# Second block: ones, low parts, sums and statistics placed anew; last routing: scaling on ScalarE

## The reference

```
x = x + _L0_xattn_ref(_layernorm(x), ctx, ctx, mask, Wq, Wk, Wv, Wo)      # 16 heads
x = x + _L0_ffn_ref(_layernorm(x), gate_w, fc_w, proj_w)                  # best 2 of 8 experts, gelu
x = x + _L1_xattn_ref(_layernorm(x), ctx, ctx, Wq, bq, Wk, bk, Wv, bv)    # one head
x = x + _L1_ffn_ref(_layernorm(x), Wr, br, W1, b1, W2, b2)                # 8 experts, dense, gated by the best 2
x = x + _L2_xattn_ref(_layernorm(x), ctx, Wq, Wkv, Wout, bout)
x = x + _L2_ffn_ref(_layernorm(x), w1, conv_w, conv_b, w2)                # ternary weights, convolution
x = x + _L3_xattn_ref(_layernorm(x), ctx, ctx, mask, Wq, bq, ..., Wo, bo)
x = x + _L3_ffn_ref(_layernorm(x), w_gate, w_gate_up, w_down)             # best 2 of 8 experts, silu(g) * u
```

## Time and profile before

| | us |
|---|---|
| runs | 600.94, 597.98, 601.21 |
| median | 600.94 |
| the profiled execution | 604.28 |
| its span, first to last instruction | 602.5 |

### The profile page before, as it was taken

How to read it: one execution, slowest core, us unless ns; L and a number is a source line. 1 busy time by engine, 2 the same in 40 slices (tenths; PEclk the granted TensorE clock), 3 DMA queues, 4 the chain that set the end, 5 groups by cost and what they waited for, 6 DMA issues and landing times.

```text
span 602.5 us, 12300 instructions
## 1 busy us (share of the span) xinstructions
PE 543.9 (90%) x3794; PEld 458.7 (76%) x3809; DVE 401.4 (67%) x1443; ACT 239.3 (40%) x551; POOL 280.1 (46%) x521
## 2 busy tenths in 40 slices
PE   5999984769999799999999999999996897999992
PEld 3678744669997498889987877767773697899992
DVE  8978853333356795465789899988887654555573
ACT  3555503345553543434444334365521222343330
POOL 4474378867657106910000050664526688644332
PEclk9999865999998999989999999999998798999997
DMA  9999012222253100000000450004001222111233
GB/s 302 377 328 274 13 53 67 68 62 75 71 167 104 64 1 1 2 0 1 1 2 0 141 140 2 1 1 141 1 1 45 67 70 58 54 46 52 79 110 122
DMA packets 48153, 47.65 MB, mean 79 GB/s; under 512 B 6471, under 2 KB 37604, under 8 KB 47943
## 3 DMA queue, kind: packets, MB, share of 16 engines
q1 hardware_dynamic: 43558, 37.68, 21.3%
q0 software_dynamic: 4544, 9.38, 4.7%
HBM read 27.53 MB, written 19.51 MB: 78 GB/s over the span
## 4 chain that ended last, share of the span: by engine, by line
PE 58%; DVE 18%; issue 11%; SPq 8%; ACT 2%; another core or an unknown queue 1%; DMA 1%; DVEq 0%; POOL 0%; POOLq 0%; ACTq 0%
PE bank L2453 18%; PE bank L2466 10%; PE bank L2027 7%; SPq L474 4%; SPq L468 2%; PE bank L2016 2%; PE bank L2017 2%; PE bank L2018 2%; PE bank L2441 2%; PE bank L2310 2%; PE bank L2223 2%; SPq L463 1%; PE bank L2268 1%; DVE X L1602 1%
## 5 line engine op out<-in xcount | busy, mean ns | idle before, releaser
L2453 PE MATMUL bank<-xT,wcur 128*128 128x128 f32 x936 | 122.7, 282 | 14.1 <-ACT xT L903 10.5
L2453 PEld LDWEIGHTS bank<-xT,wcur 128*128 128x128 f32 x936 | 114.6, 197 | 17.3 <-issue 9.4
L706 POOL DMA_INDIRECT yt<-Y,dest_i x62 | 60.3, 973 | 59.6 <-ACT Y L919 39.3
L645 POOL TENSOR_SCALAR var_eps<-mv 128x4 f32<-128x4 f32 (+2 forms) x12 | 2.9, 238 | 165.4 <-DVEq L1846 93.5
L690 POOL DMA_INDIRECT xw<-XW,slot_i x64 | 63.1, 986 | 24.6 <-issue 13.0
L1458 DVE COPY wcur<-WA 128x512 f32 x78 | 35.2, 452 | 51.1 <-PE bank L2453 37.3
L987 ACT ACTIVATE hT<-bank,b_cols 128x512 f32<-128x512 f32 x64 | 44.0, 688 | 61.4 <-PE bank L2018 60.8
L2027 PE MATMUL bank<-WC,hT 128*128 128x128 f32 x512 | 64.4, 281 | 0.0
L2027 PEld LDWEIGHTS bank<-WC,hT 128*128 128x128 f32 x512 | 62.0, 196 | 1.6 <-issue 0.2
L1473 DVE TENSOR_TENSOR hT<-gb,bank 128x512 f32<-128x512 f32 x39 | 26.8, 688 | 50.5 <-ACT gb L908 44.2
L1602 DVE SCALAR_TENSOR_TENSOR X<-bank,G,X 128x128 f32<-128x128 f32 x128 | 35.9, 345 | 29.9 <-PE bank L2027 23.5
(11 more groups left out here) (407 smaller groups left out, 1185.6 us busy)
## 6 DMA issues: line engine op xcount, KB each, us to landing
xw<-pad_rows SPq DMA_DIRECT2D x34, 260.0 KB, 4.2
xrow<-xw SPq DMA_DIRECT2D x78, 65.0 KB
WA<-in_fc_dram SPq DMA_DIRECT2D x16, 256.0 KB, 4.3
YT<-yt SPq DMA_DIRECT2D x16, 256.0 KB, 3.2
WA<-in_pj_dram SPq DMA_DIRECT2D x8, 256.0 KB, 5.9
WB<-in_fc_dram SPq DMA_DIRECT2D x8, 256.0 KB, 5.3
WB<-in_pj_dram SPq DMA_DIRECT2D x8, 256.0 KB, 6.5
X<-in_x_dram SPq DMA_DIRECT2D x2, 512.0 KB, 4.2
```

What stands on the lines that cost most here:

```text
L706: pool.indirect_dma_start(out=yt_dram, out_offset=bass.IndirectOffsetOnAxis(ap=dest_i[:, t:t + 1], axis=0), in_=y_slot(layer, t), in_offse ...
L2453: ins = pe.matmul(dst, wcur[:, s4, at:at + P], xT[s4 % 2][:, :], start=True, stop=True)
```

## The change

- TensorE issues `warm(4, 3)` at the start of `second_block`.
- `low(i)` reads PSUM and the high part, and waits for `high(i)` alone; both high copies come first, and `whole(i)` waits for `low(i)`.
- In `second_block` VectorE takes the four statistics of a batch right after adding its values.
- `weight_sums` goes from ahead of the first gates to unit 3 on VectorE, and from unit 3 to unit 6 on TensorE; `weight_scales` goes from unit 3 to unit 6, and TensorE's wait for it from unit 5 to unit 9.
- In the last routing ScalarE makes half 1's scaled tiles: `from_mean` (mean minus token) before the first exponentials, `times_root` (times the root, which GpSimd now makes with a negative sign) after them and before the two copies out of PSUM. VectorE's `ln_scaled(half(1))` stays in layer 0 alone.
- The first `warm(9, 4)` of that router becomes `warm(3, 4)`.
- Two semaphores for the masks' loads become one, `in_masks` (left out of the diff below).

```diff
@@ -640,15 +640,16 @@
-            def root(columns):
+            def root(columns, sign=1.0):
                 v, a, b = var_eps[:, columns], y_squared[:, columns], minus_half_vyy[:, columns]
...
                 for k in range(3):
+                    to = sign if k == 2 else 1.0
                     link(pool.tensor_tensor(a, y, y, ALU.mult))
                     link(pool.tensor_tensor(b, v, a, ALU.mult))
-                    link(pool.tensor_scalar(b, b, -0.5, 1.5, ALU.mult, ALU.add))
+                    link(pool.tensor_scalar(b, b, -0.5 * to, 1.5 * to, ALU.mult, ALU.add))
                     link(pool.tensor_tensor(rstd[:, columns], b, y, ALU.mult))
@@ -665,7 +666,7 @@
                 pool.wait_ge(mv_ready, 4 + 8 * a)
-                root(slice(GT, TILES))
+                root(slice(GT, TILES), (1.0, -1.0)[a])
                 pool.sem_inc(rstd_ready, 1)
@@ -857,6 +858,18 @@
+            def from_mean():
+                act.wait_ge(mv_ready, 12)
+                act.wait_ge(xn_ready, 3 * TILES + GT)
+                for t in range(GT, TILES):
+                    act.activation(XNR[:, t, :], X[:, t, :], ACT.Identity, bias=mv[:, t, 0:1], scale=-1.0).then_inc(centred, 1)
+
+            def times_root():
+                act.wait_ge(rstd_ready, 2 * GROUPS)
+                for t in range(GT, TILES):
+                    act.wait_ge(centred, t - GT + 1)
+                    act.activation(XNR[:, t, :], XNR[:, t, :], ACT.Copy, scale=rstd[:, t:t + 1]).then_inc(xn_ready, 1)
+
@@ -972,6 +985,7 @@
             def whole(i, src):
+                act.wait_ge(xd_low, i + 1)
                 act.activation(XTF[:, i % 2 * BT:(i % 2 + 1) * BT, :], four(src), ACT.Copy).then_inc(xd_out, 1)
@@ -1006,6 +1020,7 @@
                     high(i, bank[4 + i])
+                for i in range(2):
                     whole(i, bank[4 + i])
@@ -1029,8 +1044,8 @@
                         high(2, bank[6])
+                        high(3, bank[7])
                         whole(2, bank[6])
-                        high(3, bank[7])
                         whole(3, bank[7])
@@ -1100,10 +1115,12 @@
             attention(1, 2)
+            from_mean()
+            router(GROUPS)
+            times_root()
             for q in range(GB, B):
                 tokens(3, q, 4 + q)
-            for g in range(GROUPS):
-                router(GROUPS + g)
+            router(GROUPS + 1)
             experts(1)
@@ -1439,8 +1456,9 @@
                 if g == 0:
-                    dve.wait_ge(rstd_ready, GROUPS * layer + 2)
-                    ln_scaled(half(1))
+                    if layer == 0:
+                        dve.wait_ge(rstd_ready, GROUPS * layer + 2)
+                        ln_scaled(half(1))
                     first_counts(count)
@@ -1571,9 +1589,8 @@
             def low(i):
-                dve.wait_ge(xd_out, i + 1)
-                dve.tensor_tensor(XLO[i], XTF[:, i % 2 * BT:(i % 2 + 1) * BT, :].rearrange("p t c -> p (t c)"),
-                                  XH[i].bitcast(F32), ALU.subtract).then_inc(xd_low, 1)
+                dve.wait_ge(xd_high, i + 1)
+                dve.tensor_tensor(XLO[i], bank[4 + i][:, :], XH[i].bitcast(F32), ALU.subtract).then_inc(xd_low, 1)
@@ -1630,15 +1647,17 @@
                 shares1(0)
-                add1(0, bank[3])
-                add1(1, bank[0])
-                dve.wait_ge(a1_added, GB)
-                layer_norm(half(0), XNR[:, 0:GT, :], xd_ready)
+                for b, src in ((0, 3), (1, 0)):
+                    add1(b, bank[src])
+                    dve.wait_ge(a1_added, b + 1)
+                    ln_stats(everything[b * BT:(b + 1) * BT], b * BT)
+                ln_aggregate(half(0))
+                ln_rstd(GT)
+                ln_scale(half(0), XNR[:, 0:GT, :], xd_ready)
                 low(0)
...
                 combine_second(0, 1)
-                weight_sums()
                 gates1(0, bank[5])
@@ -1650,11 +1669,12 @@
                     if u == 3:
-                        weight_scales()
+                        weight_sums()
                     if u == 5:
...
                         shares1(1)
+                        weight_scales()
                     if u == 9:
@@ -2111,6 +2131,7 @@
             def second_block():
+                warm(4, 3)
                 for b in range(GB):
@@ -2134,16 +2155,15 @@
                         pe.wait_ge(d_read, 1)
-                    if u == 3:
-                        weight_sums()
                     if u == 5:
...
                         tokens1(2, bank[6])
-                        pe.wait_ge(fs_read, 1)
                         tokens1(3, bank[7])
...
                         scores1(1, bank[6])
+                        weight_sums()
                     if u == 9:
+                        pe.wait_ge(fs_read, 1)
                         turns1(2, bank[7])
@@ -2401,7 +2421,7 @@
                 else:
-                    warm(9, 4)
+                    warm(3, 4)
                 transposes(n, range(GB, B))
...
                 if layer == 0:
...
```

More of the change, by code:

```diff
@@ L347, in build @@
         zinv = sb("zinv", [P, TILES], F32)
-        in_w0, in_mask0 = (
-            sem(n) for n in ("in_w0", "in_mask0"))
+        in_w0, in_masks = (
+            sem(n) for n in ("in_w0", "in_masks"))
         in_x = [sem(f"in_x{g}") for g in range(GROUPS)]
@@ L358, in build @@
             sem(n) for n in ("const_ready", "pool_chain", "dve_chain"))
-        xn_ready, mv_ready, rstd_ready = (sem(n) for n in ("xn_ready", "mv_ready", "rstd_ready"))
+        xn_ready, mv_ready, rstd_ready, centred = (sem(n) for n in ("xn_ready", "mv_ready", "rstd_ready", "centred"))
         setup_mm, setup_evac, m_evac, ctx4_ready, mrow_ready = (
@@ L382, in build @@
         stored = sem("stored")
-        in_small, in_bias, in_rows, in_mask3, in_l2, in_ff2 = (
-            sem(n) for n in ("in_small", "in_bias", "in_rows", "in_mask3", "in_l2", "in_ff2"))
+        in_small, in_bias, in_rows, in_l2, in_ff2 = (
+            sem(n) for n in ("in_small", "in_bias", "in_rows", "in_l2", "in_ff2"))
         s1_mm, s1_evac, s2_mm, s2_act, r_mm, r_evac = (
@@ L451, in _ @@
             sp.dma_start(w0[:, :], p0).then_inc(in_w0, 16)
-            sp.dma_start(mask0_i[:, :, :], mask0).then_inc(in_mask0, 16)
+            sp.dma_start(mask0_i[:, :, :], mask0).then_inc(in_masks, 16)
             sp.dma_start(X[:, GT:TILES, :], x_v[1]).then_inc(in_x[1], 16)
@@ L564, in _ @@
             sp.wait_ge(w1_split, E)
-            sp.dma_start(mask3_i[PARTS:PARTS + K, :], mask3).then_inc(in_mask3, 16)
+            sp.dma_start(mask3_i[PARTS:PARTS + K, :], mask3).then_inc(in_masks, 16)
             sp.wait_ge(rows_out, 16)
@@ L794, in _ @@
             ins.then_inc(fs_ready, 1)
-            pool.wait_ge(in_mask3, 16)
+            pool.wait_ge(in_masks, 32)
             link(pool.tensor_scalar(mfill[0:PARTS + K, :], mask3_i, 0, FILL, ALU.is_equal, ALU.mult))
@@ L1174, in mask_values @@
             def mask_values():
-                dve.wait_ge(in_mask0, 16)
+                dve.wait_ge(in_masks, 16)
                 dve.wait_ge(cleared, 1)
```

## The result

The kernel became slower where I had forecast it faster. Four runs of each, side by side: 605.27 us median (604.57 to 606.73) after, 599.46 us (597.2 to 601.21) before, ratio 1.0104, 95% interval 1.0066 to 1.0142. The profiled execution after took 604.57 us (span 602.8 us), near its median; the one of before (604.28 us) lies 4.8 us above its median. So the spans (602.5 and 602.8 us) hide the difference, and the traces have to be compared stage by stage.

The account below looks back on a forecast made before the run. TensorE was taken to bound the kernel (58% of the chain), so savings count only where it stands still or runs slow. Gains of 1.2 + 0.1 + 0.45 + 1.38 + 1.64 = 4.8 us gave 596.1 us, range 593.0 to 601.0.

Parts of the forecast that it names:

- Part 4: Second block, weight sums and scales made later: TensorE's wait in unit 5 goes, gain 1.38 us (bounds 1.0 to 1.4).
- so nobody waits: Second block: GpSimd gets the weight scale about 12 us later, but has 93.5 us of idle time behind the dependent work.
- Part 3: Second block, low parts straight from PSUM: the first up product comes 0.45 us earlier.
- Part 1: Four products of ones ahead of the second block keep the clock full over scores and projection: gain 1.2 us.
- the first rival: The clock falls at the second block in spite of the ones: gain 3.6 us, 597.3 us; chance 0.22.
- Part 2: Second block, statistics right behind each addition fill VectorE's 0.20 us standstill: gain 0.1 us (0 to 0.2).
- Part 5: Last routing, eight scalings move from VectorE to ScalarE: the second choice starts earlier, gain 1.64 us.
- the cover thin: Last routing: scatters seen landed at 466.5, expert numbers copied at 466.7 after the change, so cover just remains.
- rival (5): The time is given back at the landings of scatters and loads for the experts: 600.5 us; chance 0.05.
- Rival (4): The last routing's table comes as late as the first's: 2.9 us slower, 603.8 us; chance 0.07.
- The sum: All five parts: 1.2 + 0.1 + 0.45 + 1.38 + 1.64 = 4.8 us, expected to reach the end.

Follow-up runs that it names:

- b_4: The kernel before with only the weight sums moved behind unit 3, scales behind unit 6, TensorE's wait to unit 9: ratio 1.0058 to the kernel before.
- b_late: The kernel before with GpSimd's mask fill waiting until VectorE has made the fourth attention addition: ratio 1.0024 to the kernel before.
- b_4gate: The kernel before with weight sums and scales moved later and GpSimd's mask fill held until the second half's scaled tiles are written: ratio 0.9998.
- a_gate: The changed kernel with GpSimd's mask fill held until the second half's scaled tiles are written: 578.54 us, ratio 1.0042 to the kernel before.
- b_3: The kernel before with only low parts read from PSUM and whole copies behind them, in both pairs: ratio 1.0006 to the kernel before.

## Why the prediction was wrong

**Part 4** failed at "so nobody waits": I asked who waits for GpSimd's results, and not whom its work slows down. The trace of before showed a 7.09 us fill behind the weight work, and VectorE's root 2.5 us behind its end; 12.9 us later (GpSimd's first step starts at 243.84 instead of 230.93) it had to lie on the root. I wrote that VectorE may run slower beside it and gave that at most 0.4 us; it measured 6.5 us in `b_4`, with the half clock behind it. The gain itself is 25.94 - 24.13 = 1.81 us in B less the 0.22 us that moved out of it, so 1.6 us (1.38 forecast).

What is slowed is told by the rows. Root steps and scalings, whose operands all lie in SBUF, stood still; the additions out of PSUM beside the fill took their usual 1.12 us (253.91 before, and 1.13 at 268.15 after). That the fill does it is shown by `b_late`, `b_4` and `b_4gate`; how it does it, only argued. The Trainium skill, "SBUF — State Buffer", Who interferes with whom, states that VectorE and GpSimd share one pair of ports as an exclusive lock, which concerns VectorE's two-port modes and its instructions with two SBUF inputs; by that rule, the traces agree: 0.17 us became 4.36, 3.86 and 1.82 us, if the one-input steps of `b_late` (3.86 and 1.82 us) ran in a two-port mode, which no row shows. Of the two-port modes the Trainium skill says there that the pair is held for the whole instruction, and these two steps waited for the very end of fill and memset. The step with two SBUF inputs (L1157) went on at 267.32 with 2.56 us of the fill left, and 0.17 us was enough for the next one at 267.75.

**Part 3** was right in the first pair (3.20 us from the transposes to the first up product became 2.76, so 0.44 us) and failed at "the second pair (u = 14) has the same order; no more than 0.1 us". There the low parts stand behind a combine on VectorE and start at 277.72, 3.16 us behind the end of the high copies, not at once; the whole copies wait for them, and the gates for the copies. It costs 1.80 us, and up to 3.35 us more when the clock falls.

**Part 1**: scores and projection came out as forecast (0.96 and 1.80 us), and VectorE's first addition came 10.20 us behind the first transpose instead of 11.42: the 1.2 us were there. They did not last. The values and the second projection took 3.58 and 3.74 us, so the second addition came 1.78 us behind the first instead of 0.90, and from the first scaling to the first up product passed 4.79 us instead of 3.60, although part 3's 0.44 us are in it. A stayed at 21.28 us. In that the first rival came true, later than it said: the clock held over the eight transposes, the scores and the projection, and fell behind them. The step that failed is "even if it holds through the projection ... I take 1.2 us", which set aside 0.57 us (its bound of 1.77 less 1.2) for what may run at half clock behind it; the values and the second projection were 3.29 us slower together. Over all runs the experiments can't tell the yield from zero.

**Part 2** was forecast at 0.1 us, since four statistics would fill a wait of 0.20 us. With the values at half clock they filled a longer one: from the second addition to the first scaling passed 4.52 us instead of 5.30, so part 2 gave back 0.78 us of what part 1 had lost. It is luck: it does so only in executions in which the values run at half clock.

**Part 5**: 1.64 us forecast and 1.64 us measured at the second choice. The failed step is that it reaches the end. I had the scatters landed at 466.5 and the numbers at 466.7 and called the cover thin; in fact, on the chips of the experiments, the loads wait for the landings of the first ten scatters, as the eleventh does 20.9 us behind the first choice, and part 5 doesn't touch that. That is rival (5), though its 600.5 us, with nearly the whole gain given back, follows from no row: only part 5's 1.64 us could go there. That an early table can cost, through ones that run out, was no rival. Rival (4) stands in the trace after as a 3.70 us wait for the table (0.86 before); in the traces of the other chips the table's wait is absent with part 5 and without it, so the change by itself doesn't make it. On the first chip the table was what came last: the loads started 1.29 us (before) and 1.06 us (after) behind the expert numbers, and the first expert product came 28.23 and 27.50 us behind the first choice, so 0.73 us of the 1.64 arrived there.

**The sum**: of 4.8 us some 2.0 were real (1.6 + 0.44), 1.2 were won and lost again within A, 1.64 went to a chain that takes little or nothing of it, and 7.7 us were lost at a place that the change doesn't name: C, D and E took 24.14 us before and 31.84 us after.

## What to carry to other kernels

When work is moved to an engine or later on it, lay its whole tail over the other engines' new times, and look for the neighbours that it slows down, not only for those who wait for the result. When two copies swap places behind a new wait, read every call of the helper: what is at once in the first pair may stand behind a queue in the second. And a gain ahead of a serial chain of scatters is worth only what that chain's start gains; if it lets filler products end early, it can cost (0.6 to 2.7 us here).

## What the runs showed of the hardware

- A step of 0.17 us on VectorE stood 4.36 us beside a GpSimd instruction of 7.10 us, and 3.86 us up to the end of one; a GpSimd memset held another for 1.82 us. The 4.36 us ended 2.56 us ahead of the GpSimd instruction's end, and steps of the same kind then took 0.17 us beside it.
- One TensorE wait of 1.64 us was followed by 6.8 us of half clock in `a_gate`, and one of 1.65 us by none in `b_3`.
- The same kernel took 599 us on one chip and 575 to 578 us on others. From the first to the last product of the first experts 87.5 us (before) and 89.8 us (after) passed in the traces there, 76.9 to 82.2 us here. The last experts tell nothing of the chip: 117.1 us in the trace of before, but 110.3 us after on the same chip, and 108.5 to 111.3 us here.
- Table entries that TensorE had made reached VectorE after waits of up to 7.0 us there, and of at most 0.83 us here.
